# Attention units with the products of transposed scores and the transposes dealt out between the value products

## The chip, the cores and the metric

The kernel runs on one core of a Trainium2 chip. The metric is the device time of one execution in microseconds. The kernel before takes 2456.54 us, the median of three runs (2456.31 to 2457.43).

## The reference, cut to what matters

A graph network on 1024 nodes of width 512: a normalization and a graph convolution at either end, and between them four layers (L = 4), each with cross-attention and a gated feed-forward part. The change is in the attention. In each layer:

```python
xb = _ln(h).reshape(BS, n // BS, d)             # BS = 16 batches of 64 nodes
q = (xb @ Wq).reshape(BS, -1, H, DH)            # 8 heads of 64
k = (cond @ Wk).reshape(BS, -1, H, DH)          # cond: 16 batches of 256 rows
v = (cond @ Wv).reshape(BS, -1, H, DH)
att = einsum('bnhd,bmhd->bhnm', q, k) * DH ** -0.5
w = softmax(att, axis=-1)
o = einsum('bhnm,bmhd->bnhd', w, v).reshape(BS, -1, H * DH)
h = h + (o @ Wo).reshape(n, d)
```

## The kernel before, in words

Each operand of a product is kept as two fp32r parts, `hi` (rounded by ScalarE) and `lo` (the rest, by VectorE or GpSimd), and a product is three matmuls for each 128 rows of contraction: hi x hi, hi x lo, lo x hi (`product`, L1867, matmuls on L1872 to L1874).

A layer's attention is 8 groups (two batches, 128 nodes each) of 4 units (a pair of heads, p = 0 to 3), 32 units in all, numbered u. The loop over layers and the one over pairs of groups are loops on the engines, and within them the order on each engine is the order in which the code issues. Engines wait for each other by counting semaphores alone. TensorE's unit u (`unit`, L2255) issues in this order:

1. `k_product` of u + 1, 12 matmuls of 512 columns. In p = 1 `wo_product` of the group before follows (12 more), in p = 3 `q_transpose`.
2. `pv_product` of u - 1 (L2117): the values of that pair times the transposed scores pT, 8 matmuls, four with v_hi of 256 columns (L2127, L2132) and four with v_lo of 128 columns (L2130). It waits for pT (`pT_ok`) and for the bank to be read (`o_part_ok`).
3. `v_product` of u + 3 (L2087), 12 matmuls of 512 columns. It waits until the bank is read (`v_ok`), and in p = 1 for the low part of cond (`c_lo`).
4. `p_transpose` of u (L2108): four 128x128 transposes of the normalized scores p_norm (L2113). It waits for p_norm (`pn_ok`).
5. `s_product` of u + 1, the scores: 6 matmuls of 256 columns. In p = 1 `t2` of the next group's z (L2140) follows, in p = 2 `q_product`.

Around it, ScalarE (unit on L930) does: p_exp of u (L938), kT_hi (L882), in p = 0 oT_hi (L905), v_hi (L878), pT's high part (L961), and at its end in p = 1 xT_hi of the next group (L886). VectorE (unit on L1597) does: rinv and p_norm of u (L1591, L1594), kT_lo (L1544), in p = 1 the residual into h and the statistics (L1643), the sum of the product with transposed scores into o_full (L1573, `o_part`), v_lo (L1539), in p = 1 z and h with the bias (L1650, L1658), pT's low part (L1628), the maxima nmx of u + 1 (L1585), and in p = 1 four writes of full for the next group (L1551). Each engine takes its instructions strictly in that order.

The units that differ: the first of a layer has no k_product and no pv_product. The last group (`last`) has no value product in p = 1, 2 and 3, and transposes z3 (`t3`, L2162) and begins the feed-forward part there; the unit before it, p = 0 of the last group (`opens_last`), has `t3(0)` ahead of pv_product and `t3(1)` between the value product and p_transpose.

Of the kernel before, what the change touches and what calls it, by code (L numbers as in the profile page):

```python
# [5 lines left out]
def gnn_preln_kernel(  # L6
# [28 lines left out]
    P = 128  # L35
# [55 lines left out]
    with ExitStack() as ctx:  # L91
        def sb(name, shape, dt, where=ctx):
            return where.enter_context(nc.sbuf_tensor(name, shape, dt))

        def sem(name):
            return ctx.enter_context(nc.semaphore(name))
# [7 lines left out]
        ident = sb("ident", [P, P], f32)  # L104
# [66 lines left out]
        cond_hi, cond_lo, xT3_hi, xT3_lo = cond[0::2], cond[1::2], xT3[0::2], xT3[1::2]  # L171
# [91 lines left out]
        def xs_of(use, t):  # L263
            return xs_2[:, t, :] if use else (xs_a, xs_b)[t // (NT // 2)][:, t % (NT // 2), :]

        ps = ctx.enter_context(nc.psum_tensor("ps", [P, 8, 512], f32))
        sums = ps[:, :, :].rearrange("p a n -> p (a n)")
        K_BANK, V_BANK, S_BANK, T_BANK, PV_BANK, X_BANK, Y_BANK = 0, 1, 2, 3, 4, 6, 7
# [44 lines left out]
        v_mm, v_hi_ok, v_ok = sem("v_mm"), sem("v_hi_ok"), sem("v_ok")  # L313
        s_mm, mx_ok, exp_ok, rinv_ok, pn_ok = (sem("s_mm"), sem("mx_ok"), sem("exp_ok"), sem("rinv_ok"),
                                               sem("pn_ok"))
        t_mm, pT_hi_ok, pT_ok, pv_mm = sem("t_mm"), sem("pT_hi_ok"), sem("pT_ok"), sem("pv_mm")
# [5 lines left out]
        o_part_ok = sem("o_part_ok")  # L322
# [1543 lines left out]
        def _(pe):  # L1866
            def product(bank, steps, first=True, last=True):  # L1867


                n = len(steps)  # L1870
                for i, (l_hi, l_lo, r_hi, r_lo) in enumerate(steps):
                    pe.matmul(bank, l_hi, r_hi, start=(first and i == 0), stop=False)  # L1872
                    pe.matmul(bank, l_hi, r_lo, start=False, stop=False)  # L1873
                    end = pe.matmul(bank, l_lo, r_hi, start=False, stop=(last and i == n - 1))  # L1874
                return end
# [4 lines left out]
            for b in range(NT):  # L1880
                last = pe.matmul(ps[:, 0, b:b + 1], ind[:, b, :], ones16[:, 0:1], start=True, stop=True)
# [16 lines left out]
            for half in range(2):  # L1898
                part = slice(4 * half, 4 * half + 4)
                pe.matmul(ps[:, 2 + half, :], before[:, :], ind[:, part, :].rearrange("p b n -> p (b n)"),  # L1900
                          start=True, stop=False)
                last = pe.matmul(ps[:, 2 + half, :], ones16[:, :], upto[:, part, :].rearrange("p b n -> p (b n)"),
                                 start=False, stop=True)
# [18 lines left out]
            for c in range(CHUNKS):  # L1922
# [4 lines left out]
                for a in range(2):  # L1927
                    last = pe.matmul(ps[:, a, 0:SLOTS + 1], codes[:, :, 1 - a], oh_d[:, c % RING, 0:SLOTS + 1],
                                     start=(c == 0), stop=(c == CHUNKS - 1))
# [4 lines left out]
                if c == G_FIRST:  # L1934
                    pe.wait_ge(d_oh_ok, 1)
                    pe.wait_ge(d_apart_ok, 2)
                    for e in range(CHUNKS):
                        last = pe.matmul(ps[0:32, 2, 0:32], d_low[:, e, :], d_high[:, :, e], start=(e == 0),
                                         stop=(e == CHUNKS - 1))
# [5 lines left out]
                if c in range(G_FIRST, G_FIRST + G_STEP * NT, G_STEP):  # L1945
                    t = (c - G_FIRST) // G_STEP
# [25 lines left out]
            for j in range(FLUSH * FLUSHES):  # L1972
# [6 lines left out]
                n, slot = CHUNKS + j, j % RING  # L1979
                s_place, d_place = ring_of(j)  # L1980
                if coded_by_scalar(j):
# [3 lines left out]
                          start=False, stop=False, skip_group_check=True).then_inc(oh_used, 1)  # L1985
# [93 lines left out]
            with pe.Fori(0, L) as l:  # L2079
# [7 lines left out]
                def v_product(u, mc, slot, bank=V_BANK):  # L2087


                    if u is not None:  # L2090
                        pe.wait_ge(v_ok, u)
                    r = slice(mc * P, (mc + 1) * P)
                    product(ps[:, bank, :], [(cond_hi[slot][:, k, r], cond_lo[slot][:, k, r],
                                                w_hi[:, 2, k, :], w_lo[:, 2, k, :])
                                               for k in range(KC)]).then_inc(v_mm, 1)
# [12 lines left out]
                def p_transpose(u):  # L2108
                    pe.wait_ge(pn_ok, u + 1)
                    for b in range(2):  # L2110
                        for c in range(2):
                            i = 2 * b + c
                            last = pe.transpose(ps[:, T_BANK, i * P:(i + 1) * P], pn[:, b, c * P:(c + 1) * P],  # L2113
                                                ident[:, :])
                    last.then_inc(t_mm, 1)

                def pv_product(u, p, slot):  # L2117


                    pe.wait_ge(pT_ok, u + 1)  # L2120

                    pe.wait_ge(o_part_ok, u + 1)
                    for b in range(2):
                        both = ps[:, PV_BANK + p % 2, b * 2 * P:(b + 1) * 2 * P]
                        upper = ps[:, PV_BANK + p % 2, b * 2 * P:b * 2 * P + P]
                        r = slice(p * P, (p + 1) * P)
                        pe.matmul(both, v_hi[:, slot, 2 * b, r], pT[:, 2 * b, :, :].rearrange("p t n -> p (t n)"),  # L2127
                                  start=True, stop=False)
                        for c in range(2):
                            pe.matmul(upper, v_lo[:, slot, 2 * b + c, r], pT[:, 2 * b + c, 0, :],  # L2130
                                      start=False, stop=False)
                        last = pe.matmul(both, v_hi[:, slot, 2 * b + 1, r],  # L2132
                                         pT[:, 2 * b + 1, :, :].rearrange("p t n -> p (t n)"),
                                         start=False, stop=True)
                    last.then_inc(pv_mm, 1)

                def t2(g, place=z2):
                    pe.wait_ge(z2_ok, g + 1)
                    for k in range(KC):
                        last = pe.transpose(ps[:, X_BANK, k * P:(k + 1) * P], place[:, k * P:(k + 1) * P], ident[:, :])  # L2140
                    last.then_inc(t2_mm, 1)
# [15 lines left out]
                def wo_product(g):  # L2157
                    pe.wait_ge(o_ok, g + 1)
                    product(ps[:, Y_BANK, :], [(oT_hi[:, p, :], oT_lo[:, p, :], w_hi[:, 3, p, :], w_lo[:, 3, p, :])
                                               for p in range(PAIRS)]).then_inc(wo_mm, 1)  # L2160
# [94 lines left out]
                def unit(u, g, p, par, last=False, first=False, opens_last=False, group0=False):  # L2255


                    if not (first or last and p == 3):
                        k_product(u + 1, (p + 1) % 4, par if p < 3 else 1 - par)
                    if opens_last:  # L2260
                        t3(0)
                    if p == 1 and not group0:
                        wo_product(g - 1)
                    if p == 3 and not last:
                        q_transpose(g + 1)
                    if p == 3 and last:

                        pe.wait_ge(w_ok, FIRST_PIECES + PIECES * l + 2)
                        pe.wait_ge(x3_ok, 2 + NT * l + 2)
                        mlp_product(0, 0, 0, 0, slice(0, 2 * P))  # L2270
                    if not first:
                        pv_product(u - 1, (p + 3) % 4, par if p else 1 - par)
                    if p == 1 and not last:

                        wait_apart(pe, c_lo, 2 * (g + 1) + 2)
                    if not (last and p >= 1):
                        v_product(u + 3, (p + 3) % 4, par if p == 0 else 1 - par)
                    if opens_last:
                        t3(1)
                    if p == 2 and last:  # L2280
                        t3(3)
                    if p == 3 and last:

                        pe.wait_ge(full3_ok, NT * l + 4)
                        mlp_product(0, 0, 0, 1, slice(0, 2 * P))
                    p_transpose(u)
                    if not (last and p == 3):
                        s_product(u + 1, g if p < 3 else g + 1, (p + 1) % 4)
                    if p == 2 and not last:
                        q_product(g + 1)  # L2290
                    if p == 1 and not last:
                        t2(g + 1)
                    if p == 1 and last:

                        pe.wait_ge(v_ok, UNITS * l + UNITS)
                        t3(2)
                    if p == 2 and last:
                        t3(4)
                    if p == 3 and last:
                        t3(5)  # L2300

                        pe.wait_ge(x3_ok, 2 + NT * l + 4)
                        mlp_product(0, 0, 0, 0, slice(2 * P, HALF))
# [84 lines left out]
            for t in range(NT):  # L2388
                pe.wait_ge(h_ffo, 64 * L - NT + t + 1)
                for k in range(KC):  # L2390
                    last = pe.transpose(ps[:, t, k * P:(k + 1) * P], h[:, t, k * P:(k + 1) * P], ident[:, :])
# [56 lines left out]
```

## Time and profile before

| | |
|---|---|
| runs, median | 2456.54 us |
| the profiled execution | 2454.11 us, its span 2452.2 us |
| TensorE matmul | 2393.9 us, 98% of the span, 12215 instructions |
| TensorE weight load | 1980.2 us, 81% |
| VectorE | 1675.5 us, 68% |
| ScalarE | 1132.2 us, 46% |
| GpSimd | 689.7 us, 28% |
| granted TensorE clock, mean | 0.992 |

Busy time is the sum of an engine's instructions without their overlap. A matmul's recorded duration contains its way through the array, and the next one starts before it ends, so its pace is read from the distance of starts and not from durations. Weight loads have rows of their own (PEld).

### The profile page before, as it was taken

Reading aid. Unit: us, or ns where it says so; the run is one execution under the profiler, and the core shown is the slowest. Engines: PE = TensorE matmul, PEld = TensorE weight load, DVE = VectorE, ACT = ScalarE, POOL = GpSimd, SP = SyncE. Lnnn points to the kernel's source line nnn. Section 1 sums busy time; section 2 is a strip of 40 time slices with the busy share of each in tenths; the row PEclk is TensorE's granted clock in tenths of the full one; section 3 lists DMA queues with packets and bytes.
Section 4 is the critical chain, followed back from the end, with each engine's and each line's share of the span. In section 5 each row is a group of like instructions: output and inputs, shape, how many; then the busy total and the mean of one; then the engine's idle time right before and its main releaser. Section 6 shows DMA issues by size and latency. Waiting matters only on the chain.

```text
span 2452.2 us, 37083 instructions
## 1 busy us (share of the span) xinstructions
PE 2393.9 (98%) x12215; PEld 1980.2 (81%) x12215; DVE 1675.5 (68%) x3202; ACT 1132.2 (46%) x2280; POOL 689.7 (28%) x521
## 2 busy tenths in 40 slices
PE   6879999999999999999999999999999999999999
PEld 5448888888888888888888888888888888878887
DVE  8896776776555776675565676675666677675566
ACT  8974443554334344554334434554334434644332
POOL 3000000156641000156541000066550000066541
PEclk8989999999999999999999999999999999999999
DMA  2021000112211000112211000122211000022122
GB/s 78 1 95 48 35 17 35 35 52 70 70 65 45 35 34 18 35 52 78 69 65 36 35 34 18 35 63 76 69 57 38 33 34 25 28 71 76 61 80 97
DMA packets 82646, 122.44 MB, mean 50 GB/s; under 512 B 5808, under 2 KB 63536, under 8 KB 77872
## 3 DMA queue, kind: packets, MB, share of 16 engines
q1 hardware_dynamic: 82480, 120.32, 14.6%
q8 instruction: 93, 1.52, 0.3%
q14 instruction: 73, 0.60, 0.1%
HBM read 116.10 MB, written 4.19 MB: 49 GB/s over the span
## 4 chain that ended last, share of the span: by engine, by line
PE 83%; DVE 10%; issue 3%; ACT 3%; POOL 1%; DMA 0%; DVEq 0%; POOLq 0%; ACTq 0%; SPq 0%
PE ps L1872 18%; PE ps L1873 17%; PE ps L1874 17%; PE ps L2191 7%; PE ps L2195 7%; PE ps L2193 7%; PE ps L2113 2%; PE ps L2130 2%; PE ps L2132 2%; DVE oh_d L1382 1%; PE ps L2127 1%; DVE z L1735 1%; DVE w_lo L1740 1%; ACT z L911 1%; PE ps L1994 1%
## 5 line engine op out<-in xcount | busy, mean ns | idle before, releaser
L550 POOL TENSOR_SCALAR veps<-mv 128x1 f32<-128x1 f32 x65 | 17.3, 266 | 1003.3 <-DVE mv L1176 1003.3
L1808 DVE TENSOR_TENSOR h<-h,ps 128x512 f32<-128x512 f32 x256 | 168.7, 683 | 66.3 <-PE ps L1874 66.3
L632 POOL TENSOR_TENSOR f_lo<-ff,f_hi 128x512 fp32r<-128x512 f32 x128 | 167.3, 1317 | 164.8 <-ACT f_hi L1062 164.8
L1872 PE MATMUL ps<-cond_hi,w_hi 128*128 128x512 f32 x512 | 203.6, 398 | 0.0
L1872 PE MATMUL ps<-w_hi,cond_hi 128*128 128x512 f32 x512 | 200.9, 392 | 0.5 <-POOL w_lo L557 0.3
L1874 PE MATMUL ps<-w_hi,cond_lo 128*128 128x512 f32 x512 | 200.0, 391 | 0.0
L1873 PE MATMUL ps<-cond_lo,w_hi 128*128 128x512 f32 x512 | 200.0, 391 | 0.0
L1874 PE MATMUL ps<-cond_hi,w_lo 128*128 128x512 f32 x512 | 200.0, 391 | 0.0
L1873 PE MATMUL ps<-w_lo,cond_hi 128*128 128x512 f32 x512 | 199.7, 390 | 0.0
L1872 PE MATMUL ps<-wf_hi,f_hi 128*128 128x512 f32 x512 | 199.6, 390 | 0.0
L1873 PE MATMUL ps<-wf_lo,f_hi 128*128 128x512 f32 x512 | 199.2, 389 | 0.0
L1874 PE MATMUL ps<-wf_hi,f_lo 128*128 128x512 f32 x512 | 199.2, 389 | 0.0
L878 ACT ACTIVATE v_hi<-ps 128x512 fp32r<-128x512 f32 x128 | 76.4, 597 | 259.1 <-PE ps L1874 259.0
L2191 PE MATMUL ps<-xT_hi,wg_hi 128*128 128x512 f32 x480 | 188.4, 393 | 3.8 <-DVE ff L1725 3.2
L2195 PE MATMUL ps<-xT_hi,wg_lo 128*128 128x512 f32 x480 | 186.9, 389 | 0.0
L2193 PE MATMUL ps<-xT_lo,wg_hi 128*128 128x512 f32 x480 | 186.9, 389 | 0.0
L1539 DVE TENSOR_TENSOR v_lo<-ps,v_hi 128x512 fp32r<-128x512 f32 x128 | 88.5, 691 | 118.7 <-ACT v_hi L878 117.9
L938 ACT ACTIVATE p_exp<-ps,nmx 128x256 f32<-128x256 f32 x256 | 118.4, 468 | 102.0 <-DVE nmx L1585 101.4
L1062 ACT ACTIVATE f_hi<-ff 128x512 fp32r<-128x512 f32 x128 | 81.0, 633 | 170.7 <-DVE ff L1787 97.4
L652 POOL TENSOR_TENSOR wg_lo<-stage,wg_hi 128x768 fp32r<-128x768 f32 x56 | 106.9, 1908 | 107.9 <-DVE sums_s L1761 107.9
L1591 DVE RECIPROCAL rinv<-rsum 128x2 f32<-128x2 f32 x128 | 21.2, 166 | 162.0 <-ACT p_exp L938 162.0
L1074 ACT ACTIVATE gel<-gel,cols_sb 128x512 f32<-128x512 f32 x104 | 75.3, 724 | 114.3 <-DVE gel L1775 111.1
(308 smaller groups left out, 6709.1 us busy)
## 6 DMA issues: line engine op xcount, KB each, us to landing
stage<-in_pieces SPq DMA_DIRECT2D x82, 512.0 KB, 3.3
stage<-in_condT SPq DMA_DIRECT2D x33, 1024.0 KB, 4.8
stage<-in_pieces SPq DMA_DIRECT2D x224, 128.0 KB, 2.6
x<-in_x SPq DMA_DIRECT2D x2, 1024.0 KB, 6.6
at_s<-at SPq DMA_DIRECT2D x1, 2048.0 KB, 6.2
at16b<-at_s SPq DMA_DIRECT2D x1, 2048.0 KB, 11.1
out<-h SPq DMA_DIRECT2D x8, 256.0 KB, 2.0
bias_row<-in_rows SPq DMA_DIRECT2D x6, 256.0 KB, 3.4
```

The source lines that it names most:

```text
L632: pool.tensor_tensor(f_lo[q % 2][:, c, half * HALF:(half + 1) * HALF], ff[:, s % 2, :], bits(f_hi[q % 2][:, c, half * HALF:(half + 1) * HA ...
L652: pool.tensor_tensor(lo[:, 0:3, :], stage[:, r % 2, 256:1024].rearrange("p (b n) -> p b n", n=256), bits(hi[:, 0:3, :]), ALU.subtract)
L938: e = act.activation(pe_[:, b, :], ps[:, S_BANK, b * M:(b + 1) * M], ACT.Exp, bias=nmx[:, b:b + 1], accum_out=rsum[:, b:b + 1])
L1062: act.activation(f_hi[q % 2][:, c, half * HALF:(half + 1) * HALF], ff[:, s % 2, :], ACT.Copy)\
L1539: dve.tensor_tensor(v_lo[:, slot, mc, :], ps[:, bank, :], bits(v_hi[:, slot, mc, :]), ALU.subtract).then_inc(v_ok, 1)
L1808: dve.tensor_tensor(h[:, t, :], h[:, t, :], ps[:, down_bank(q, t), :], ALU.add)\
L1872: pe.matmul(bank, l_hi, r_hi, start=(first and i == 0), stop=False)
L1873: pe.matmul(bank, l_hi, r_lo, start=False, stop=False)
L1874: end = pe.matmul(bank, l_lo, r_hi, start=False, stop=(last and i == n - 1))
L2191: pe.matmul(ps[:, bank, :], hi[:, a, r], moving[0][:, n, :], start=(first and n == 0), stop=False, skip_group_check=True)
L2193: pe.matmul(ps[:, bank, :], hi[:, a, r], moving[1][:, n, :], start=False, stop=False, skip_group_check=True)
L2195: last = pe.matmul(ps[:, bank, :], lo[:, a, r], moving[0][:, n, :], start=False, stop=(n == 1), skip_group_check=True)
```

## The change: what it does

In the units that have both a product with transposed scores and a value product, TensorE no longer issues these one after the other. A new function deals them: the 12 matmuls of the value product, behind each of the first 8 one matmul of pv_product, and behind each of the last 4 one transpose of p_transpose. Numbers, shapes, operands and banks of the matmuls are the same. The waits move along: first `v_ok`; behind the first value matmul those for `pT_ok` and `o_part_ok`; behind the ninth that for `pn_ok`; in p = 1 `c_lo` now stands ahead of all. The semaphores of the results are raised with the eighth product with transposed scores, the twelfth value matmul and the fourth transpose. In the unit that opens the last group the transposes now come ahead of `t3(1)`. The first unit of a layer and the last three keep the old order.

```diff
+                def v_pv_transposes(u, p, par):
+
+                    v, slot = (p + 3) % 4, par if p == 0 else 1 - par
+                    rows = slice(v * P, (v + 1) * P)
+                    pv_bank, pv_slot, pair = PV_BANK + v % 2, par if p else 1 - par, slice(v * P, (v + 1) * P)
+
+                    def v_part(i):
+                        j, part = i // 3, i % 3
+                        return pe.matmul(ps[:, V_BANK, :], (cond_hi, cond_hi, cond_lo)[part][slot][:, j, rows],
+                                         (w_hi, w_lo, w_hi)[part][:, 2, j, :], start=(i == 0), stop=(i == 11))
+
+                    def pv_part(i):
+                        b, j = i // 4, i % 4
+                        if j in (0, 3):
+                            c = 2 * b + j // 3
+                            return pe.matmul(ps[:, pv_bank, b * 2 * P:(b + 1) * 2 * P], v_hi[:, pv_slot, c, pair],
+                                             pT[:, c, :, :].rearrange("p t n -> p (t n)"), start=(j == 0), stop=(j == 3))
+                        c = 2 * b + j - 1
+                        return pe.matmul(ps[:, pv_bank, b * 2 * P:b * 2 * P + P], v_lo[:, pv_slot, c, pair],
+                                         pT[:, c, 0, :], start=False, stop=False)
+
+                    def t_part(i):
+                        b, c = i // 2, i % 2
+                        return pe.transpose(ps[:, T_BANK, i * P:(i + 1) * P], pn[:, b, c * P:(c + 1) * P], ident[:, :])
+
+                    pe.wait_ge(v_ok, u + 3)
+                    for i in range(12):
+                        v_end = v_part(i)
+                        if i == 0:
+
+                            pe.wait_ge(pT_ok, u)
+                            pe.wait_ge(o_part_ok, u)
+                        if i < 8:
+                            pv_end = pv_part(i)
+                            if i == 7:
+                                pv_end.then_inc(pv_mm, 1)
+                        else:
+                            if i == 8:
+                                pe.wait_ge(pn_ok, u + 1)
+                            if i == 11:
+                                v_end.then_inc(v_mm, 1)
+                            t_end = t_part(i - 8)
+                    t_end.then_inc(t_mm, 1)
...
-                    if not first:
+                    if p == 1 and not last:
+
+                        wait_apart(pe, c_lo, 2 * (g + 1) + 2)
+                    mixed = not first and not (last and p >= 1)
+                    if mixed:
+                        v_pv_transposes(u, p, par)
+                    elif first:
+                        v_product(u + 3, (p + 3) % 4, par if p == 0 else 1 - par)
+                    else:
                         pv_product(u - 1, (p + 3) % 4, par if p else 1 - par)
-                    if p == 1 and not last:
-
-                        wait_apart(pe, c_lo, 2 * (g + 1) + 2)
-                    if not (last and p >= 1):
-                        v_product(u + 3, (p + 3) % 4, par if p == 0 else 1 - par)
                     if opens_last:
                         t3(1)
...
-                    p_transpose(u)
+                    if not mixed:
+                        p_transpose(u)
```

## Rows read from the trace of the kernel before

**Rows 1.** The page, part 1: busy time, share of the span, instructions.

```profile
PE 2393.9 (98%) x12215; PEld 1980.2 (81%) x12215; DVE 1675.5 (68%) x3202; ACT 1132.2 (46%) x2280; POOL 689.7 (28%) x521
```

**Rows 2.** Table by stretch: length, then PE, PEld, DVE, ACT, POOL busy, clock, DMA.

```profile
222.67:468.91 246.24, 246.24 (x1351) 211.88 (x1350) 169.93 (x354) 102.34 (x240) 18.43 (x31) 1.00 0.07 26
```

**Rows 3.** Timeline, weight loads, unit p = 1 of a middle group: start, duration, what.

```profile
442.30 0.30 PEld L2130 LDWEIGHTS ps<-pT,v_lo 128*128 128x128 f32 x2
442.52 0.19 PEld L2132 LDWEIGHTS ps<-pT,v_hi 128*128 128x128 f32 x1
...
443.21 0.19 PEld L1873 LDWEIGHTS ps<-w_lo,cond_hi 128*128 128x128 f32 x1
443.45 0.19 PEld L1874 LDWEIGHTS ps<-w_hi,cond_lo 128*128 128x128 f32 x1
443.69 0.19 PEld L1872 LDWEIGHTS ps<-w_hi,cond_hi 128*128 128x128 f32 x1
443.92 0.19 PEld L1873 LDWEIGHTS ps<-w_lo,cond_hi 128*128 128x128 f32 x1
...
445.50 0.19 PEld L1874 LDWEIGHTS ps<-w_hi,cond_lo 128*128 128x128 f32 x1
445.73 0.59 PEld L2113 LDWEIGHTS ps<-ident,p_norm 128*128 128x128 f32 x4
446.29 0.19 PEld L1872 LDWEIGHTS ps<-kT_hi,qbd_hi 128*128 128x128 f32 x1
```

**Rows 4.** Timeline, ScalarE and VectorE, the chain to the next p_norm.

```profile
446.16 0.60 ACT L878 ACTIVATE v_hi<-ps 128x512 fp32r<-128x512 f32 x1 [5.16 <-PE ps L1874]
446.79 0.69 DVE L1539 TENSOR_TENSOR v_lo<-ps,v_hi 128x512 fp32r<-128x512 f32 x1 [1.70 <-ACT v_hi L878]
...
449.77 1.36 DVE L1551 TENSOR_SCALAR full<-ps,cols_sb 128x128 f32<-128x128 f32 x4
...
451.17 0.63 ACT L886 ACTIVATE xT_hi<-full 128x512 fp32r<-128x512 f32 x1 [3.92 <-DVE full L1551]
...
452.94 0.64 DVE L1594 TENSOR_SCALAR p_norm<-p_exp,rinv 128x256 f32<-128x256 f32 x2
```

**Rows 5.** Timeline, weight loads of the transposes in p = 2.

```profile
453.75 0.59 PEld L2113 LDWEIGHTS ps<-ident,p_norm 128*128 128x128 f32 x4
```

**Rows 6.** The same pair, first (layer 0, group 1) and last (layer 3, group 6).

```profile
270.11 0.64 DVE L1594 TENSOR_SCALAR p_norm<-p_exp,rinv 128x256 f32<-128x256 f32 x2
...
270.92 0.14 PEld L2113 LDWEIGHTS ps<-ident,p_norm 128*128 128x128 f32 x1
...
2094.05 0.65 DVE L1594 TENSOR_SCALAR p_norm<-p_exp,rinv 128x256 f32<-128x256 f32 x2
...
2094.86 0.14 PEld L2113 LDWEIGHTS ps<-ident,p_norm 128*128 128x128 f32 x1
```

**Rows 7.** Timeline, weight loads, first unit of the first layer.

```profile
218.38 0.19 PEld L1874 LDWEIGHTS ps<-w_hi,cond_lo 128*128 128x128 f32 x1
218.94 0.42 PEld L2113 LDWEIGHTS ps<-ident,p_norm 128*128 128x128 f32 x4 [0.37 <-DVE p_norm L1594]
219.33 0.19 PEld L1872 LDWEIGHTS ps<-kT_hi,qbd_hi 128*128 128x128 f32 x1
```

**Rows 8.** Timeline, the pair in p = 0 and in p = 2 of group 0.

```profile
432.12 0.62 DVE L1594 TENSOR_SCALAR p_norm<-p_exp,rinv 128x256 f32<-128x256 f32 x2
...
435.45 0.14 PEld L2113 LDWEIGHTS ps<-ident,p_norm 128*128 128x128 f32 x1
...
232.36 0.63 DVE L1594 TENSOR_SCALAR p_norm<-p_exp,rinv 128x256 f32<-128x256 f32 x2
...
234.35 0.37 PEld L2113 LDWEIGHTS ps<-ident,p_norm 128*128 128x128 f32 x2
```

**Rows 9.** Timeline, the last group: z of t3(1) on ScalarE, the residual.

```profile
473.42 1.51 ACT L911 ACTIVATE z<-ps,cols_sb 128x128 f32<-128x128 f32 x4
...
479.93 0.69 DVE L1643 TENSOR_TENSOR h<-h,ps 128x512 f32<-128x512 f32 x1
```

More of the change, by code:

```diff
@@ L2270, in unit @@
                         mlp_product(0, 0, 0, 0, slice(0, 2 * P))
-                    if not first:
-                        pv_product(u - 1, (p + 3) % 4, par if p else 1 - par)
                     if p == 1 and not last:
                         wait_apart(pe, c_lo, 2 * (g + 1) + 2)
-                    if not (last and p >= 1):
+                    mixed = not first and not (last and p >= 1)
+                    if mixed:
+                        v_pv_transposes(u, p, par)
+                    elif first:
                         v_product(u + 3, (p + 3) % 4, par if p == 0 else 1 - par)
+                    else:
+                        pv_product(u - 1, (p + 3) % 4, par if p else 1 - par)
                     if opens_last:
```

## The prediction

> **What bounds the kernel now.** I read the page first. TensorE is busy 98% of the span at full granted clock [rows 1]. Then the table by stretch: in the attention groups of the first layer TensorE's busy time equals the stretch itself, 246.24 of 246.24 us, while VectorE is at 69% and ScalarE at 42% [rows 2]. So in attention two things can move the time: how densely TensorE is fed, and a wait that now does not exist but nearly does. For the first I read the weight loads in order of time, because the start of a load is the sharpest clock here: each load begins as the matmul before it starts to stream, so the distance of two loads is what one matmul occupies. For the second I followed one group's softmax chain across ScalarE and VectorE and compared its end with the load that waits for it.
>
> What the loads say [rows 3]: a 512-column matmul takes 0.227 us (445.73 less 443.21, eleven of them, is 2.52). The two 128-column products with v_lo take 0.11 each (442.30 to 442.52). The four transposes and the step after them take 0.56 from 445.73 to 446.29: 0.23 is the last value product, so a transpose takes 0.11. A 256-column one takes 0.12. A 128-column matmul is only a quarter of a 512-column one and yet costs half of it: something other than its columns holds it.
>
> What the chain says: in the p = 2 unit p_norm ends at 452.94 + 0.64 = 453.58 [rows 4] and the first transpose's load goes at 453.75 [rows 5]. The slack is 0.17. This repeats in every p = 2 unit of groups 1 to 6 in all four layers: first and last of the 24 are shown, 270.75 against 270.92 and 2094.70 against 2094.86 [rows 6]. Nothing waits there today, but only just.
>
> **The change part by part.** A layer has 32 units. The first and the last three are left as they are, so 28 x 4 = 112 units are dealt anew. In each, 12 value products (512 columns), 8 products with transposed scores (four of 256 columns, four of 128) and 4 transposes keep their number and shapes. Nothing is removed; only order changes.
>
> (a) The 12 small ones behind a value product. Can the load of their neighbour hide? The price of a small matmul between two large ones is bounded by two rows. Where the array had run dry, the first transpose started 0.06 after its load (four transposes' loads at 218.94, the next load at 219.33: 0.39, less three at 0.11) [rows 7]. That is the low end: 0.06, a saving of 0.05 on each of the eight 128-column ones, 0.40 us a unit. The high end is 0.12, the 256-column pace. The nearest rows speak for 0.11, no change: the first transpose of every unit already stands right behind a value product, whose 0.227 gave its own load all the time it wanted, and it still takes 0.11 until the next; and the last transpose, with the load of a larger product behind it, takes 0.11 as well [rows 3]. It is the load of the next matmul, begun when the small one starts, that takes 0.11, and a large product behind needs the same 128x128 load. I take 0.11: 0 gained. The four 256-column ones cover that load already.
>
> The Trainium skill speaks for a gain: "TensorE: Matmul & The Clock Gate", section "Architectural detail: the array is 16× 32×32, not 1× 128×128", says that the engine's queue can pull weight loads ahead of matmuls in flight, and its section "Back-to-back issue gap" gives about 81 ns per 128-column matmul in a sustained stream. No row here shows 81. At that price the eight would save 0.23 us a unit, 26 us in all, which would cancel the losses below.
>
> (b) The value products. Behind a small one a large one goes slower: after the last product of transposed scores the loads of the value products stand 0.24, 0.24 and 0.23 apart, against 0.227 later [rows 3]. Summed over eleven the excess is 2.52 - 11 x 0.227 = 0.02 us. Dealt out, each of eleven stands behind a small one. Low end 0: 0.02 less than now. High end 0.013 on each: 0.14 - 0.02 = 0.12. I take 0.0075, between them and nearer to what the three together show per product: 0.08 - 0.02 = 0.06 us a unit, 6.7 us in 112 (ends -2 and +13).
>
> (c) The wait for p_norm. The first transpose moves from behind the twelfth value product to behind the ninth: three products earlier, 0.68. By (b), eight of the products ahead of it are 0.04 longer together, and the p = 2 unit begins 0.06 later because p = 1 is longer. Its load could go at 453.75 - 0.68 + 0.04 + 0.06 = 453.17. The other side gets later. p_norm of p = 2 hangs on the value products of p = 1: v_hi at 446.16 follows their last one directly, v_lo follows v_hi, then without a gap on VectorE z, h, pT, the maxima and four full; xT_hi stands on ScalarE ahead of p_exp [rows 4]. In the new order three transposes (0.33) and the excess (0.06) stand ahead of the last value product, so the chain ends 0.39 later, at 453.97; with 0.05 for the semaphore the load goes at 454.02, 0.85 late. Queued behind it on TensorE are three value products, three transposes and the next unit, everything. Not all of the delay is lost. In each layer's first unit this wait exists today: the load went at 218.94, and without a wait it would have gone 0.23 after the one at 218.38, so it was 0.33 late. From 218.38 to the load behind the transposes it took 0.95; a unit without the wait takes 0.79 (445.50 to 446.29). So 0.16 of the delay was lost, and about 0.16 was hidden under the last value product [rows 3, 7]. The stall is 0.85 - 0.16 = 0.69 us, in 24 units 16.6 us. Low end: the chain keeps its time (0.30, 7 us); high end: nothing hidden (0.85, 20 us).
>
> The other units have room. In p = 0 p_norm ends at 432.74 and its load goes at 435.45 [rows 8]: 2.7, and p = 1 and p = 3 have more. In p = 2 of group 0 the chain lacks the residual and z: 232.99 against 234.35 [rows 8], 1.36 less 0.68 less 0.39 plus 0.10, no wait.
>
> (d) The other waits that move. Those for pT and o_full now come behind the first value product, 0.23 later: no cost. The end of the products with transposed scores comes 1.8 us later, and VectorE's o_full reduction stands ahead of v_lo in its queue; but v_lo waits for the value products anyway, which end later still (1.70 us of idle is there today [rows 4]), so it costs nothing. If that cover went, the reduction would stand in the chain in (c) with its own length. The wait for cond_lo in p = 1 moves ahead by 0.92; cond_lo is written before p_norm of that unit, a unit's length ahead. No DMA is issued by TensorE, and none hangs on these steps.
>
> (e) The last unit that is dealt anew opens the last group. There the transposes t3(1) of z3 came ahead of p's and now come behind: ScalarE's z, at 473.42 [rows 9], starts about 0.4 later, after v_hi and t3(1). VectorE works without a gap from there into the last three units, which wait for it; the residual at 479.93 [rows 9] waited for TensorE and gives 0.1 back. I take 0.3 in each layer, 1.2 us (ends 0 and 0.5 each, 0 to 2).
>
> Sum: 0 + 6.7 + 16.6 + 1.2 = 24.5 us. The profiled execution took 2454.11 us (its span 2452.2 and 1.9 around it), 2.4 below the median of the runs, 2456.54. 2454.1 + 24.5 = 2478.6, and by the median 2481.0.
>
> **The rivals.** What this kernel's measurement can tell from no change is 0.2%, 4.9 us.
>
> First, the other side: the load behind a small matmul hides. Place: the eight 128-column ones of each unit; price 0.06 instead of 0.11, 0.40 us a unit, 44.8 us less. The stall grows, for the p = 2 transposes come 0.2 earlier still and its unit 0.4 earlier while the chain gains 0.35: 0.94 each, 22.6. With 6.7 and 1.2 the sum is -14.3: 2442. It decides from 0.032 us saved per small one: the 896 of them save 896 x 0.032, the stalls give 24 x 5 x 0.032 of it back, and what is left is the 24.5 us of losses. For it: the start 0.06 after the load [rows 7], and a pace that columns don't explain. Against it: that start had an idle array, and behind a value product the transpose keeps 0.11 [rows 3]. 0.12. Half hidden, at 0.08 each, 0.03 saved, it is 24.5 - 776 x 0.03 = 1.2 us: 2458, no difference, 0.03. (That price is about where the Trainium skill's figure, in (a), stands; by its 81 ns it is 2458.5.)
>
> Second, switching costs more than in (b): at the top of its range (13), and the twelve small ones at 0.12 (0.01 x 12 x 112 = 13). With the stalls and (e) that is 44: 2500. Against: the transitions in rows 3 come at 0.11 without exception. 0.09.
>
> Third, the chain isn't late by what I say, because the three transposes cost the last value product less: stall 0.3. 7 + 6.7 + 1.2 = 15: 2471. 0.08.
>
> **How the numbers follow.** The forecast has 0.68. Its own ends are 2456.5 + 5 and + 35, where all low or all high ends fall together, which they hardly do; 2468 to 2490 holds most of it. The range of 2466 to 2491 takes in the third rival, and leaves out the first, most of the second and the tails. Faster by over 0.2%: the first rival, 0.12. Within 0.2%: 0.03. Slower: 0.85.
>
> **What would show it.** Right: TensorE idle ahead of the transposes, put down to p_norm, some 0.7 to 0.85 us in 24 units of p = 2 and in none of p = 0, 1 and 3 apart from each layer's first unit; loads behind a small matmul 0.11 apart, behind a value product 0.23; p_norm of p = 2 0.4 later in its group. Attention of a layer some 6 us longer, the feed-forward part unchanged. Wrong: small ones at 0.06 to 0.08, or no such waits, or a unit of p = 3 (no stall in it) that is longer or shorter by more than 0.1.

## The result and the profile after

The changed kernel takes 2480.22 us (median of 4 runs, 2479.74 to 2480.88) against 2456.43 for the kernel before (median of 4 too, 2455.76 to 2457.43): the ratio is 1.0099, 95% interval 1.0087 to 1.0111. It is 23.8 us slower. Forecast were 2481.0, and 24.5 more than before. Its profiled execution has a span of 2479.0 us.

The page of the changed kernel, part 1:

```profile
PE 2405.5 (97%) x12215; PEld 1972.3 (80%) x12215; DVE 1678.0 (68%) x3202; ACT 1129.9 (46%) x2280; POOL 689.9 (28%) x521
```

The instructions are as many as in [rows 1]; the span grew and TensorE's share fell. Who waited for whom (us in total, times, longest), TensorE's matmuls first, then its weight loads:

```profile
PE ps L2160 <- DVE p_norm L1594: 11.8, 24, 0.5
...
PE ps L2113 <- DVE p_norm L1594: 3.5, 4, 0.9
```

```profile
PEld ps L2160 <- DVE p_norm L1594: 19.4, 24, 0.8
```

L2160 is the transpose in the dealt order. It waits for p_norm 24 times, and the other row (L2113, the transposes left in the old order) stands as before. Weight loads (start, duration, what) of p = 1 of the same middle group as in [rows 3]:

```profile
448.81 0.19 PEld L2145 LDWEIGHTS ps<-w_lo,cond_hi 128*128 128x128 f32 x1
448.93 0.19 PEld L2155 LDWEIGHTS ps<-pT,v_lo 128*128 128x128 f32 x1
449.16 0.19 PEld L2145 LDWEIGHTS ps<-w_hi,cond_lo 128*128 128x128 f32 x1
449.26 0.19 PEld L2155 LDWEIGHTS ps<-pT,v_lo 128*128 128x128 f32 x1
449.50 0.19 PEld L2145 LDWEIGHTS ps<-w_hi,cond_hi 128*128 128x128 f32 x1
...
451.59 0.19 PEld L2145 LDWEIGHTS ps<-w_hi,cond_hi 128*128 128x128 f32 x1
451.72 0.14 PEld L2160 LDWEIGHTS ps<-ident,p_norm 128*128 128x128 f32 x1
451.93 0.19 PEld L2145 LDWEIGHTS ps<-w_lo,cond_hi 128*128 128x128 f32 x1
```

Read as in the prediction, a load begins when the matmul before it starts. So 448.93 to 449.16 is a value product (0.23, the next 449.26 to 449.50 is 0.24), and 449.16 to 449.26 is a 128-column matmul (0.11 with the rounding; over all 448 places the mean is 0.108). At a transpose the split is another one: 0.13 for the transpose (451.59 to 451.72; the median of 336 is 0.133) and 0.21 for the value product behind it (451.72 to 451.93).

The reading holds to 2 to 4 ns for most matmuls, but not for a value product behind a 128-column one. The matmul records of the same place:

```profile
449.15 0.22 PE L2155 MATMUL ps<-pT,v_lo 128*128 128x128 f32 x1
449.21 0.45 PE L2145 MATMUL ps<-w_hi,cond_lo 128*128 128x512 f32 x1
```

By its record the value product starts 0.06 after the small one, at 449.21, and 0.05 before the load behind it goes at 449.26 (median of 448 places 0.051; behind a transpose 0.108). How a pair's time is split between its two matmuls thus depends on which start is read. The time of the pair does not: a product with v_lo and the value product behind it take 0.108 + 0.236 = 0.344, a transpose and the value product behind it about 0.343, while the two kinds in rows of their like take 0.227 + 0.108 = 0.335. Nothing of a pair is saved.

The p = 2 unit behind that p = 1, loads, with the idle time before them in brackets; then the chain to its p_norm on ScalarE and VectorE:

```profile
459.29 0.19 PEld L2145 LDWEIGHTS ps<-w_hi,cond_lo 128*128 128x128 f32 x1
460.29 0.14 PEld L2160 LDWEIGHTS ps<-ident,p_norm 128*128 128x128 f32 x1 [0.81 <-DVE p_norm L1594]
460.29 0.25 PEld L2145 LDWEIGHTS ps<-w_hi,cond_hi 128*128 128x128 f32 x1
```

```profile
452.81 0.60 ACT L878 ACTIVATE v_hi<-ps 128x512 fp32r<-128x512 f32 x1 [5.03 <-PE ps L2145]
453.45 0.69 DVE L1539 TENSOR_TENSOR v_lo<-ps,v_hi 128x512 fp32r<-128x512 f32 x1 [1.03 <-ACT v_hi L878]
...
456.44 1.36 DVE L1551 TENSOR_SCALAR full<-ps,cols_sb 128x128 f32<-128x128 f32 x4
457.83 0.63 ACT L886 ACTIVATE xT_hi<-full 128x512 fp32r<-128x512 f32 x1 [3.93 <-DVE full L1551]
...
459.60 0.63 DVE L1594 TENSOR_SCALAR p_norm<-p_exp,rinv 128x256 f32<-128x256 f32 x2
```

p_norm ends at 460.23 and the load goes at 460.29. The chain itself is as long as in [rows 4]: 6.79 us from v_hi's start to p_norm's, 6.78 before. It starts later, and its end is wanted earlier. Counted from the start of unit p = 1, in the mean of the 24, p_norm of p = 2 ends 0.355 later than before, and the load behind it would be due 0.624 earlier. So it goes 0.865 late: 0.997 behind the load ahead of it, where after_chain_freed (below), without the wait, has 0.133.

For the comparisons below I took a unit's length as the distance between the ends of two successive score products, from the semaphore events in the traces. In ns beyond the kernel before (means over groups 1 to 6, four layers; the third unit of the last group is its p = 2; the last column is the sum in us over the attention of all layers, up to the last score product of each):

```
kernel                 p=3   p=0   p=1   p=2   third unit of last group   attention
changed                 72    37    31   760   318                        +23.7
pv_only                 67    40    38    29   310                         +6.2
t_only                  40    27    21   776   311                        +22.5
after_chain_freed       66    32    53    44   321                         +6.7
t_one_later             68    47    46   416   313                        +16.0
vlo_256                135    94    96   764   337                        +28.8
last_group_unit_old     73    41    28   766    -2                        +22.3
pv_in_pairs             32    48    32    35    74                         +4.6
before_chain_freed       0     0    -2     0     5                          0.0
up_low_later             0     0     1     0  -731                         -2.9
```

Outside these stretches the profiles of the changed kernel and its variants are 1.5 to 4 us longer than that of the kernel before, and before_chain_freed, whose attention takes as long as before, is too (1.9 us), so this table tells more than their spans. What happens behind the last score product of a layer it does not count; that matters in up_low_later alone.

The ratios below are to the kernel before as timed beside each experiment (medians 2455.81, and 2455.28 for up_low_later).

### The profile page after: what moved, and what is told of

The parts are those of the page before. It is cut to its first block, busy times and chain, and to the rows that moved or that the text cites. A ratio compares the mean times of both kernels' runs of the same rounds, so it can differ in the third digit from the quotient of the medians.

```text
span 2479.0 us, 37083 instructions
## 1 busy us (share of the span) xinstructions
PE 2405.5 (97%) x12215; PEld 1972.3 (80%) x12215; DVE 1678.0 (68%) x3202; ACT 1129.9 (46%) x2280; POOL 689.9 (28%) x521
## 4 chain that ended last, share of the span: by engine, by line
PE 74%; DVE 14%; issue 5%; ACT 5%; POOL 1%; DMA 1%; DVEq 0%; SPq 0%; ACTq 0%; POOLq 0%
PE ps L1872 12%; PE ps L1873 12%; PE ps L1874 12%; PE ps L2145 11%; PE ps L2235 7%; PE ps L2237 6%; PE ps L2239 6%; PE ps L2160 2%; PE ps L2152 2%; DVE full L1551 1%; DVE oh_d L1382 1%; ACT p_exp L938 1%; DVE z L1735 1%; ACT z L911 1%; DVE pT L1628 1%
## 5 line engine op out<-in xcount | busy, mean ns | idle before, releaser
L2145 PE MATMUL ps<-w_hi,cond_lo 128*128 128x512 f32 x448 | 193.4, 432 | 0.0
L2145 PE MATMUL ps<-w_lo,cond_hi 128*128 128x512 f32 x448 | 191.3, 427 | 0.0
L1573 DVE TENSOR_REDUCE o_full<-ps 64x128 f32<-64x256 f32 x256 | 107.5, 420 | 48.6 <-PE ps L2152 38.4
L2160 PE MATMUL ps<-ident,p_norm 128*128 128x128 f32 x448 | 122.7, 274 | 11.8 <-DVE p_norm L1594 11.8
```

The costliest lines, as they stand in the source:

```text
L1573: last = dve.tensor_reduce(o_full[r, p, :].rearrange("d (b n) -> d b n", b=2), o_ps[:, :, :, r].rearrange("d b t n -> d b n t"), AX.X, ALU ...
L2145: return pe.matmul(ps[:, V_BANK, :], (cond_hi, cond_hi, cond_lo)[part][slot][:, j, rows], (w_hi, w_lo, w_hi)[part][:, 2, j, :], start=(i = ...
L2160: return pe.transpose(ps[:, T_BANK, i * P:(i + 1) * P], pn[:, b, c * P:(c + 1) * P], ident[:, :])
```

## The experiments

My theory was the prediction's: small matmuls keep their price, a large one behind a small one pays a little, and the rest is a p_norm that comes too late in 24 units. The rival was that mixing as such costs, or that hidden loads gain something and a larger stall eats it.

**pv_only.** Only the products with transposed scores are dealt.

```diff
-                        else:
-                            if i == 8:
-                                pe.wait_ge(pn_ok, u + 1)
-                            if i == 11:
-                                v_end.then_inc(v_mm, 1)
-                            t_end = t_part(i - 8)
-                    t_end.then_inc(t_mm, 1)
+                        elif i == 11:
+                            v_end.then_inc(v_mm, 1)
...
-                    if not mixed:
-                        p_transpose(u)
+                    p_transpose(u)
```

> The changed kernel with only the eight products with transposed scores dealt between the value products; the four transposes stand behind the twelfth value product again, as before. My account (a large product behind a small one takes about 0.0075 us longer, a small one keeps its 0.11 us, and the rest is the wait of the p = 2 transposes for p_norm): the transposes are back in place and no transpose stands ahead of the last value product, so the slack of 0.15 us is kept but for 0.05. No wait in p = 2. Left are 8 x 0.0075 less 0.02 in 112 units, 4 to 6 us: 2461. Rival A (weight loads behind small ones do hide a little and the stall eats it): this one would be faster than the kernel before, 2445 to 2454, for the eight stand as they do in the changed kernel and the stall is gone. Rival B (the loss is in the mixing as such, spread over all units): about two thirds of the 23.8 us stay, 2472.

Measured: 2462.08 us, ratio 1.0027 (1.0016 to 1.0038). In the matmuls' rows no wait for p_norm but the four of before, in the last group's p = 2:

```profile
PE ps L2113 <- DVE p_norm L1594: 3.5, 4, 0.9
```

In the p = 2 units of groups 1 to 6 p_norm ends 0.185 us or more ahead of its load. Both rivals fall: it is slower than before, not faster, and by 6 us, not 16.

**t_only.** Only the transposes are dealt.

```diff
-                    pe.wait_ge(v_ok, u + 3)
-                    for i in range(12):
-                        v_end = v_part(i)
-                        if i == 0:
-
-                            pe.wait_ge(pT_ok, u)
-                            pe.wait_ge(o_part_ok, u)
-                        if i < 8:
-                            pv_end = pv_part(i)
-                            if i == 7:
-                                pv_end.then_inc(pv_mm, 1)
-                        else:
+                    pe.wait_ge(pT_ok, u)
+                    pe.wait_ge(o_part_ok, u)
+                    for i in range(8):
+                        pv_end = pv_part(i)
+                    pv_end.then_inc(pv_mm, 1)
+                    pe.wait_ge(v_ok, u + 3)
+                    for i in range(12):
+                        v_end = v_part(i)
+                        if i >= 8:
```

> The changed kernel with only the transposes dealt: the eight products with transposed scores stand in one piece ahead of the value products, as before, and the transposes behind the ninth to the twelfth value product. My account: the p = 2 transposes are wanted three value products earlier (0.68 us) and the chain to their p_norm starts three transposes later (0.33 us), so 24 stalls of about 0.7 us, 17 us, plus 0.3 us in each layer's last group (1.2) and some 0.03 us a unit (3): 2478. Rival A (hidden loads of small ones, which must show for the transposes too): 3 x 0.05 us saved in 112 units, 17 us, 2461. Rival B (the loss is in the mixing as such): a third of it, 2464.

Measured: 2478.59 us, ratio 1.0095 (1.0078 to 1.0112). Dealing four transposes alone costs nearly all of it:

```profile
PE ps L2160 <- DVE p_norm L1594: 12.7, 24, 0.5
```

The parts don't add up to the whole: in the table pv_only and t_only lose 6.2 + 22.5 = 28.7 us, the changed kernel 23.7. Of the 5.0 us, 1.2 are the last group's delay, which is paid once and not twice; the rest lies in all kinds of units, some 0.03 us in each, so the surcharges of the two kinds of small matmuls are not a sum either.

**after_chain_freed.** TensorE's order is the changed kernel's; xT_hi moves on ScalarE.

```diff
                     if not (first or last and p == 3):
                         k_high(u + 1)
+                    if p == 2 and not last:
+                        x2_high(g + 1)
...
-                    if p == 1 and not last:
-                        x2_high(g + 1)
```

> The changed kernel, TensorE's order untouched; on ScalarE the copy xT_hi for the next group moves from the end of unit p = 1 to behind p_exp and kT_hi of unit p = 2, so that p_exp of p = 2 no longer waits for VectorE's four writes of full. My account (the stall is the late p_norm of p = 2): p_norm comes more than 1 us earlier there, all 24 stalls of 0.7 us go, 2480.2 - 16.9 = 2463.3, and the units p = 2 are as long as p = 0 and 1 beyond before, by 0.03 to 0.05 us. Rival (the stall belongs to the place of the wait, behind the ninth value product, or to the transposes' start there): nothing moves, 2480. If a second wait stands close behind the first (q_product for xT_lo, which now comes later), it shows as a wait at q_product in p = 2 and the time falls between.

Measured: 2463.66 us, ratio 1.0031 (1.0019 to 1.0042); 16.6 us of the loss are gone without a change on TensorE (15.9 if each kernel is set against the kernel before as timed beside it, 17.0 in the table). VectorE and the load in the middle group:

```profile
454.10 0.62 DVE L1594 TENSOR_SCALAR p_norm<-p_exp,rinv 128x256 f32<-128x256 f32 x2
...
455.63 0.14 PEld L2160 LDWEIGHTS ps<-ident,p_norm 128*128 128x128 f32 x1
```

p_norm ends at 454.72, 0.91 ahead of its load. The p = 2 units fall from 760 to 44 ns beyond before, and no wait for p_norm is left there. So the stall is 0.716 us each, 17.2 in 24. (The units p = 1 are 22 ns longer than in the changed kernel; the table's total falls by 17.0 for that.)

**before_chain_freed.** The same move in the kernel before, the control.

> Control: the kernel before, with the same move on ScalarE as in the run with the freed chain (xT_hi behind p_exp and kT_hi of p = 2). My account: the chain had 0.15 us of slack in every p = 2 unit and none of it was paid, so the time stays, 2456 within 1, while p_norm of p = 2 comes more than 1 us earlier. Rival (the move is worth something by itself, so that its 16.5 us in the changed kernel don't measure the stall): faster by several us.

Measured: 2455.84 us, ratio 1.0001 (0.9991 to 1.0010). Worth nothing by itself, within 2.4 us by the runs and within 0.1 us in the attention of the profile, though p_norm of p = 2 ends 1.9 us ahead of its load instead of 0.165. So the move measures the stall alone.

**t_one_later.** The transposes start one value product later.

```diff
-                        else:
-                            if i == 8:
+                        elif i > 8:
+                            if i == 9:
...
-                            t_end = t_part(i - 8)
+                            t_end = t_part(i - 9)
+                    t_end = t_part(3)
```

> The changed kernel with the transposes one value product later: the first behind the tenth, the second behind the eleventh, the third and fourth behind the twelfth; the wait for p_norm moves along. A dose between the changed kernel and the one with only the products with transposed scores dealt. My account (stall = lateness of p_norm less 0.16 us): the first transpose is wanted 0.23 us later, and two instead of three transposes stand ahead of the last value product, so the chain ends 0.11 earlier: 0.34 us less in each of the 24 stalls of p = 2, which were 0.70. 2480.2 - 8.2 = 2472, and units p = 2 about 0.41 us longer than before instead of 0.76. Rival (a fixed price for a wait in the middle of a dealt stretch): all 24 stay, 2480; rival (the stall goes only when the transposes stand in one piece): also 2480.

Measured: 2471.63 us, ratio 1.0065 (1.0048 to 1.0082). All 24 waits are still there, but shorter:

```profile
PEld ps L2160 <- DVE p_norm L1594: 14.2, 24, 0.6
```

The p = 2 units are 416 ns beyond before instead of 760: 0.34 us less, as worked out from one value product and one transpose. The load goes 0.55 late instead of 0.865. The loss follows the place of the transposes.

**vlo_256.** Twice the columns for the four products with v_lo.

```diff
-                        return pe.matmul(ps[:, pv_bank, b * 2 * P:b * 2 * P + P], v_lo[:, pv_slot, c, pair],
-                                         pT[:, c, 0, :], start=False, stop=False)
+                        return pe.matmul(ps[:, pv_bank, b * 2 * P:(b + 1) * 2 * P], v_lo[:, pv_slot, c, pair],
+                                         pT[:, c, :, :].rearrange("p t n -> p (t n)"), start=False, stop=False)
```

> The changed kernel, but the four products with v_lo in each unit take both parts of pT, 256 columns instead of 128 (the small product of the two low parts is added to the sum; nothing is left out). 448 matmuls with twice the columns. My account (a small matmul here is held by the load of the next one, about 0.108 us, and not by its columns): each grows from 0.108 to 0.118 us, 448 x 0.010 = 4.5 us, 2484.7, or less if the large product behind it loses its small surcharge. Rival (a small one's columns are what is paid and the 0.11 is something else that stays): each grows by 128 columns at the pace of the 512-column ones, 0.227/4 = 0.057 us, 448 x 0.057 = 25 us: 2506.

Measured: 2484.22 us, ratio 1.0114 (1.0097 to 1.0131), 4.0 above the changed kernel; the rival wanted 25. The intervals of the two ratios overlap, so the runs alone don't fix the 4.0; the table gives 5.1, and the loads' distances 0.118 us for these matmuls (mean of 448) against 0.108, 4.3 us in all. The loads of the same place as above:

```profile
450.19 0.19 PEld L2155 LDWEIGHTS ps<-pT,v_lo 128*128 128x128 f32 x1
450.42 0.19 PEld L2145 LDWEIGHTS ps<-w_hi,cond_lo 128*128 128x128 f32 x1
450.54 0.19 PEld L2155 LDWEIGHTS ps<-pT,v_lo 128*128 128x128 f32 x1
```

The 256-column matmul takes 0.12 (450.42 to 450.54), the 128-column one took 0.11. Doubling the columns costs 0.010 us where the rival wanted 0.057: from 128 to 256 they are not what sets the price here. The p = 2 units hardly grow (764 against 760): there the added work lies inside the stall.

**last_group_unit_old.** The unit that opens the last group keeps the old order.

```diff
-                    mixed = not first and not (last and p >= 1)
+                    mixed = not first and not last and not opens_last
...
```

The branch behind it then issues pv_product and v_product one after the other in that unit, as before.

> The changed kernel, but the unit that opens the last group of each layer (p = 0 of group 7) keeps the old order. Read in the unit lengths of the profile: in the changed kernel the third unit of the last group is 0.31 us longer than before. My account: there the sum into o_full comes 1.85 us later, oT_hi, which waits for it, stands ahead of v_hi on ScalarE and pushes it and all behind it by 0.5, and VectorE's full queue hands 0.35 of it on to the three last units. With the old order there: that unit back to its length within 0.03, four times 0.32 and four times 0.05 us less, 1.5 us, too little for the runs' times. Rival (the last group is late because the layer as a whole is shifted against the loads of the feed-forward weights): the 0.31 us stay.

Measured: 2478.07 us in one run; the third unit of the last group is back at its old length (-2 ns instead of 318). ScalarE there, the changed kernel first, then this one:

```profile
478.22 0.63 ACT L917 ACTIVATE xT_hi<-z 128x512 fp32r<-128x512 f32 x1
480.05 0.63 ACT L905 ACTIVATE oT_hi<-o_full 128x512 fp32r<-128x512 f32 x1 [1.20 <-DVE o_full L1573]
480.59 0.58 ACT L878 ACTIVATE v_hi<-ps 128x512 fp32r<-128x512 f32 x1
```

```profile
477.85 0.63 ACT L917 ACTIVATE xT_hi<-z 128x512 fp32r<-128x512 f32 x1
478.39 0.61 ACT L905 ACTIVATE oT_hi<-o_full 128x512 fp32r<-128x512 f32 x1
479.66 0.60 ACT L878 ACTIVATE v_hi<-ps 128x512 fp32r<-128x512 f32 x1 [0.66 <-PE ps L1874]
```

In the changed kernel oT_hi waits 1.20 us for o_full and v_hi, wanted by everything behind, stands in the queue after it. With the old order oT_hi is done early and v_hi waits for TensorE alone. The dose fits as well: in pv_in_pairs the products with transposed scores end 0.2 us earlier than in pv_only, and that unit is 0.074 us beyond before instead of 0.310.

**pv_in_pairs.** As pv_only, two small ones behind every second value product.

```diff
-                        if i < 8:
-                            pv_end = pv_part(i)
-                            if i == 7:
+                        if i < 8 and i % 2 == 0:
+                            for n in (i, i + 1):
+                                pv_end = pv_part(n)
+                            if i == 6:
...
```

> As the run with only the eight products with transposed scores dealt, but two behind every second value product, four places instead of eight. Read in the loads' distances. My account (a large product that stands behind a small one takes some 0.008 us longer, per such place): four places instead of eight, so a p = 3 unit is longer than before by about 0.03 instead of 0.067 us, and a small one stays at 0.108 (128 columns) and 0.117 (256). Rival (the surcharge is per small product or per change of accumulation bank in total): it stays at 0.067 or falls otherwise than with the places.

Measured: 2460.86 us in one run. The p = 3 units halve as expected (32 against 67 ns), but p = 0 rises from 40 to 48, and over a group of four units the surcharge falls from 174 to 147 ns, not to half. That it goes by the number of places is not shown; what sets it stays open.

**up_low_later.** An attempt to gain from the waits that are there without the change, in the kernel before.

```diff
                         k_low(u + 1)
+                    if p == 2 and last:
+                        up_low(1)
...
-                    if p == 1 and last:
-                        up_low(1)
                     if p in (2, 3) and last:
```

> The kernel before, TensorE's order untouched; on VectorE the low part of the second up-projection piece (1.2 us) moves in the last group from unit p = 1, where it stands ahead of z, pT and the maxima, to unit p = 2 behind kT_lo. It goes for the waits that are there without the change: the longest one for p_norm, 0.88 us in each layer's last p = 2 unit. My account (VectorE's queue is what the last three units wait for): p_norm there comes about 0.9 us earlier and most of that wait goes; xT_lo and pT of the next unit then come later by part of it, so that 0.4 to 0.9 us a layer is left, 1.6 to 3.6 us: 2453 to 2454.5. Rival (ScalarE's z of t3 holds that chain anyway): nothing, 2456.

Measured: 2455.09 us, ratio 0.9996 (0.9987 to 1.0005): no difference. Up to the last score product of each layer there is a gain of 0.73 us, and the waits for p_norm fall from 3.5 us to

```profile
PE ps L2113 <- DVE p_norm L1594: 1.1, 4, 0.3
```

but the time does not follow. The very next unit gives most of it back: there the products with transposed scores wait for pT's low part (L1628), which stands behind the moved instruction in VectorE's queue. Their wait in the kernel before, and then in this one:

```profile
PE ps L2127 <- DVE pT L1628: 0.7, 4, 0.2
```

```profile
PE ps L2127 <- DVE pT L1628: 2.7, 8, 0.5
```

By the loads this wait takes 0.57 us more in each layer, 0.70 against 0.12, so that 0.15 of the 0.73 us is left, 0.6 us in four layers, which these runs can't tell from nothing. The expectation had the mechanism and put what is left too high, at 0.4 to 0.9. No version here beats the kernel before.

## Why the prediction was right, point by point

(a) Small matmuls: 0 forecast, and no saving found. Behind a value product and ahead of one, the 128-column products took 0.108 us over 448 places, as in [rows 3], and never less; vlo_256 shows that twice the columns add 0.010. The transposes did not come 0.11 apart from what follows, as the prediction had it, but 0.133, with a value product of 0.21 behind them; the pair is 0.008 dearer than its parts and not cheaper. The prediction's clock, "each load begins as the matmul before it starts to stream", was too simple here: by the matmul records the value product does start some 0.06 behind the small one, as at the idle array [rows 7], but the time of the pair does not shrink by it. (The 81 ns that the Trainium skill gives in "TensorE: Matmul & The Clock Gate", section "Back-to-back issue gap", and that the prediction weighed, were not met at any of these places: the least of the 448 is 0.108.)

(b) The surcharge: forecast 0.06 us in 112 units, 6.7. Measured in the 88 units without a stall 0.047, and 0.044 in the 24 of p = 2 where after_chain_freed shows it bare: 88 x 0.047 + 24 x 0.044 = 5.2. That is 1.5 us less than forecast. What sets it is open: it is no fixed price per place (pv_in_pairs, t_only).

(c) The stall: forecast 0.69 us in 24 units, 16.6. Measured 0.760 - 0.044 = 0.716, 17.2. The load was forecast 0.85 late and went 0.865 late; the chain ended 0.355 later where 0.39 was forecast, and the load was due 0.62 earlier where 0.58 was, two small errors that nearly cancel. The rule read from each layer's first unit, delay less 0.16, held: 0.865 late and 0.716 lost leave 0.15 hidden, and t_one_later, 0.55 late and 0.416 - 0.044 = 0.372 lost, leaves 0.18. The units named as free of a stall are free of it, p = 2 of group 0 too, whose p_norm has 0.37 us of slack left (0.39 by the prediction's figures).

(e) The last group: forecast 1.2 us, measured 4 x 0.318 = 1.3, but the step that led there was wrong in part. It put the delay down to t3(1) standing behind the transposes. In pv_only t3(1) and the transposes keep their order, and 0.31 us is lost all the same. There it is step (d) that failed, "so it costs nothing": the later end of the products with transposed scores holds up o_full, which holds oT_hi, which stands ahead of v_hi on ScalarE. (d) looked at VectorE's queue only. In the other p = 0 units the same delay meets slack: p_norm of p = 1 is still 3.2 us early there. In t_only the products are early and the third unit is 0.31 us longer too, so the other route costs as much by itself: v_hi waits for the value products, which end behind three transposes, and starts 0.36 us later than before (0.55 in pv_only; first layer, counted from the unit's start). The two run side by side and don't add up. That the forecast for (e) came out although (d) had missed one of them is luck.

The sum of the measured terms is 5.2 + 17.2 + 1.3 = 23.7. They come from the table, so that they meet its +23.7 says only that no kind of unit was left out; the check from outside is the 23.8 of the runs. The forecast's 24.5 is a little too much surcharge and a little too little stall.

## What to carry to other kernels

Where matmuls on TensorE carry 128 columns or fewer, ask first what load stands behind them: moving them next to large ones gained nothing here; by the loads' order the one behind a small matmul began only when the small one started. Before an instruction is moved forward, write down the slack of what it waits for in every kind of unit, and add what the same move pushes ahead of that chain's own start: here 0.68 us less and 0.39 us later met a slack of 0.17, in one unit of four, and made 17 of the 24 us. And when a result comes later, look through the queue of every engine that reads it or what is made of it, not only the first.

## What the runs showed of the hardware

Twice the columns (256 for 128) cost a dealt matmul 0.010 us, as expected of it: 0.118 against 0.108 by the loads. Not expected: between two products with transposed scores a 512-column matmul takes 0.230 to 0.238 us by the same reading, against 0.227 in a row of its like, and between two transposes 0.210, where the transposes take 0.133 instead of 0.108. Its own record starts up to 0.11 us before the load behind it. No run here shows what that is.
